# Cross-attention and gated feed-forward on one core: where the first keys are masked, how queries are normalised, and when the statistics are taken

## The reference, cut to what matters

```python
def _layernorm(x, axis=-1, eps=1e-05):
    m = jnp.mean(x, axis=axis, keepdims=True)
    v = jnp.var(x, axis=axis, keepdims=True)
    return (x - m) / jnp.sqrt(v + eps)
...
    qk = jnp.einsum('bhdq,bhdl->bhql', qh, kh) * scale
    sm = jax.nn.softmax(qk, axis=-1)
    ret = jnp.einsum('bhql,bhdl->bhdq', sm, vh)
...
    x = x + jnp.tanh(g_xattn[0]) * _L0_xattn_ref(_layernorm(x, axis=-1), ctx_2048, ctx_2048, L0_xattn_gamma)
    x = x + jnp.tanh(g_ffn[0]) * _L0_ffn_ref(_layernorm(x, axis=-1), ...)
```

## Time and profile before

| what | value |
|---|---|
| median of 3 runs | 214.7 us (214.63 to 214.72) |
| profiled execution, its own time | 213.49 us |
| span of its instructions | 211.7 us |
| mean granted clock of TensorE | 0.974 of full speed |
| busy: PE, DVE, POOL, ACT | 198.6, 159.3, 145.7, 125.0 us |

### The profile page before, as it was taken

How to read it: one execution, slowest core, us unless ns; L and a number is a source line. 1 busy time by engine, 2 the same in 40 slices (tenths; PEclk the granted TensorE clock), 3 DMA queues, 4 the chain that set the end, 5 groups by cost and what they waited for, 6 DMA issues and landing times.

```text
span 211.7 us, 4722 instructions
## 1 busy us (share of the span) xinstructions
PE 198.6 (94%) x1785; PEld 120.9 (57%) x1785; DVE 159.3 (75%) x336; ACT 125.0 (59%) x242; POOL 145.7 (69%) x167
## 2 busy tenths in 40 slices
PE   8569999999999999999999998999799999999991
PEld 5236456665665566556654553446566666766581
DVE  3799899999999997698968617055957676765985
ACT  2012758776877586768776774369547544854450
POOL 5994779957999999983799302384554899567440
PEclk9975899999999999999999999999999999999999
DMA  6799601101122231232311412311320003003033
GB/s 177 228 351 388 125 2 53 31 26 49 53 91 70 65 127 31 59 117 67 101 58 50 121 39 55 102 51 51 113 90 10 2 3 99 0 0 99 5 99 99
DMA packets 19783, 17.75 MB, mean 84 GB/s; under 512 B 4016, under 2 KB 19248, under 8 KB 19760
## 3 DMA queue, kind: packets, MB, share of 16 engines
q1 hardware_dynamic: 19760, 17.44, 26.6%
HBM read 11.02 MB, written 6.42 MB: 82 GB/s over the span
## 4 chain that ended last, share of the span: by engine, by line
PE 79%; DVE 12%; ACT 3%; issue 2%; POOL 1%; DMA 1%; SPq 0%; DVEq 0%; ACTq 0%; POOLq 0%
PE ps L727 19%; PE ps L791 17%; PE ps L768 13%; PE ps L739 12%; PE ps L852 9%; DVE neg_max L545 6%; PE ps L742 4%; PE ps L755 2%; PE ps L752 2%; ACT p_t L468 1%; DMA c_sb<-in_ctx 1%; PE ps L778 1%; ACT xn L497 1%; DVE p_t L701 1%; DVE p_t L696 1%
## 5 line engine op out<-in xcount | busy, mean ns | idle before, releaser
L545 DVE TENSOR_REDUCE neg_max<-ps 128x2 f32<-128x512 f32 x128 | 79.5, 683 | 11.8 <-PE ps L727 11.6
L468 ACT ACTIVATE p_t<-ps 128x512 f32<-128x512 f32 x128 | 66.9, 600 | 20.9 <-PE ps L742 18.9
L727 PE MATMUL ps<-km,qn 32*128 32x512 f32 x256 | 74.6, 651 | 3.7 <-POOL qn L351 3.2
L739 PE MATMUL ps<-qm,c_sb 32*128 32x512 f32 x256 | 74.6, 651 | 1.3 <-ACT p_t L468 1.3
L791 PE MATMUL ps<-w_exp,w_gu 128*128 128x512 f16 x192 | 45.2, 380 | 1.3 <-DVE w_exp L596 1.2
L434 POOL TENSOR_TENSOR f_lo<-fu,f_hi 128x512 fp32r<-128x512 f32 x23 | 29.3, 1279 | 21.5 <-ACT f_hi L486 21.5
L742 PE MATMUL ps<-max_t,sel 4*128 4x256 bf16 x256 | 35.1, 274 | 0.0
L742 PEld LDWEIGHTS ps<-max_t,sel 4*128 4x128 bf16 x256 | 18.8, 96 | 23.1 <-issue 20.7
L768 PE MATMUL ps<-p_t,v_t 128*32 128x256 f32 x512 | 30.9, 382 | 0.4 <-ACT p_t L468 0.4
L662 DVE SCALAR_TENSOR_TENSOR ga<-th,ps 128x512 f32<-128x512 f32 x24 | 16.4, 682 | 19.6 <-ACT th L481 19.6
L739 PEld LDWEIGHTS ps<-qm,c_sb 32*128 32x128 f32 x256 | 27.3, 188 | 5.8 <-issue 2.9
(11 more groups left out here) (69 smaller groups left out, 228.1 us busy)
## 6 DMA issues: line engine op xcount, KB each, us to landing
u_scr<-u_sb SPq DMA_DIRECT2D x32, 128.0 KB
u_n<-u_scr SPq DMA_DIRECT2D x16, 128.0 KB
r_n<-r_scr SPq DMA_DIRECT2D x16, 128.0 KB
out_x<-p_t SPq DMA_DIRECT2D x16, 128.0 KB, 1.9
x_sb<-in_x SPq DMA_DIRECT2D x3, 512.0 KB, 8.9
c_sb<-in_ctx SPq DMA_DIRECT2D x3, 512.0 KB, 8.9
w_all<-in_L_ffn_gate_w SPq DMA_DIRECT2D x1, 768.0 KB, 9.2
w_all<-in_L_ffn_up_w SPq DMA_DIRECT2D x1, 768.0 KB, 9.8
```

The lines of the kernel that those rows point to most:

```text
L468: nc.scalar.activation(p_t[:, b % 2, i, :], ps[:, bank_of["t", n][0], :], ACT.Exp, scale=DH ** -0.5).then_inc(exp_ok, 1)
L545: nc.vector.tensor_reduce(neg_max[:, b % 2, at:at + PAR, 0], ps[:, bank_of["s", n][0], :].rearrange("p (e l) -> p e l", e=PAR), axis=AX.X, ...
L727: nc.tensor.matmul(ps[:, bank, :], qn[rows, b % 2, P * t:P * (t + 1)], km[rows, b % 2].rearrange("p e l -> p (e l)"), start=True, stop=Tru ...
L739: nc.tensor.matmul(ps[:, bank, :], c_sb[rows, b, P * t:P * (t + 1)], qm[rows, b % 4].rearrange("p e l -> p (e l)"), start=True, stop=False)
```

## The change

Masking the first keys moves from POOL to DVE, which also computes the negated mean of batch 0; `km` of batch 0 has a semaphore of its own (`k0_ok`). POOL computes negated means for the later groups inside `pow_group` and normalises by adding the negated mean, where it subtracted the mean; `norm_apply_first` likewise uses the negated means of the second norm, which were there before. The masked queries become a function of their own, `masked(b)`; in the opening, `masked(0)` stands behind `queries(1)` and the clearing of `nm_parts`, and `masked(1)` behind the clearing of `v_t`. DVE's statistics are taken by the table `STATS`, for one to three batches at a time; `binades` and `rounded` get other steps, the scale products go from step 9 to step 11, and `pick` and `sel` stand behind the first keys. PE does 20 products ahead of the first scores, where it did 25.

```diff
--- before.py
+++ after.py
@@ -29,8 +29,9 @@
 E4M3_MIN_EXP = 2.0 ** -6
 E4M3_MAGIC = 1.5 * 2.0 ** 20
 HALF = HT * I // 2
-HALF_BINADES = (1, 2, 4, 5, 6, 8)
-HALF_ROUNDED = (2, 3, 5, 6, 7, 8)
+STATS = {0: (4, 6), 1: (6, 8), 4: (8, 11), 5: (11, 14), 7: (14, 15), 9: (15, 16)}
+HALF_BINADES = (2, 3, 6, 8, 9, 10)
+HALF_ROUNDED = (3, 4, 6, 8, 10, 11)
 
 
 def bank_table():
@@ -117,6 +118,7 @@
 
         stats = sb("stats", [P, NB, 6])
         mv = sb("mv", [P, NB, 2])
+        neg_m = sb("neg_m", [P, NB])
         veps = sb("veps", [P, NB])
         rstd = sb("rstd", [P, NB])
         stats2 = sb("stats2", [P, NB, 6])
@@ -186,8 +188,11 @@
         ag1_ok = sem("ag1_ok")
         v1_ok = sem("v1_ok")
         r1_ok = sem("r1_ok")
+        nm0_ok = sem("nm0_ok")
+        nm1_ok = sem("nm1_ok")
         qn_ok = sem("qn_ok")
         qm_ok = sem("qm_ok")
+        k0_ok = sem("k0_ok")
         k_ok = sem("k_ok")
         s_ok = sems("s_ok", NG)
         max_ok = sem("max_ok")
@@ -334,6 +339,8 @@
                 nc.gpsimd.tensor_scalar(veps[:, lo:hi], mv[:, lo:hi, 1], EPS, None, ALU.add).then_inc(v1_ok, 1)
                 pool.wait_ge(v1_ok, n + 1)
                 nc.gpsimd.tensor_tensor(rstd[:, lo:hi], veps[:, lo:hi], mhalf[:, 0:hi - lo], ALU.pow).then_inc(r1_ok, 1)
+                if n > 0:
+                    nc.gpsimd.tensor_scalar(neg_m[:, lo:hi], mv[:, lo:hi, 0], -1.0, None, ALU.mult).then_inc(nm1_ok, 1)
 
             def keys(b):
                 pool.wait_ge(masks_ok, 1)
@@ -346,10 +353,17 @@
 
             def queries(b):
                 pool.wait_ge(r1_ok, group_of(b) + 1)
+                if group_of(b) > 0:
+                    pool.wait_ge(nm1_ok, group_of(b))
+                else:
+                    pool.wait_ge(nm0_ok, 1)
                 if b >= 2:
                     pool.wait_ge(max_ok, FILLS * (b - 1))
-                nc.gpsimd.tensor_scalar(qn[:, b % 2, :], x_sb[:, b, :], mv[:, b, 0:1], rstd[:, b:b + 1],
-                                        ALU.subtract, ALU.mult).then_inc(qn_ok, 1)
+                nc.gpsimd.tensor_scalar(qn[:, b % 2, :], x_sb[:, b, :], neg_m[:, b:b + 1], rstd[:, b:b + 1],
+                                        ALU.add, ALU.mult).then_inc(qn_ok, 1)
+
+            def masked(b):
+                pool.wait_ge(masks_ok, 1)
                 if b >= 4:
                     pool.wait_ge(exp_ok, FILLS * (b - 3))
                 pool.wait_ge(qn_ok, b + 1)
@@ -357,16 +371,18 @@
                     nc.gpsimd.tensor_scalar(qm[:, b % 4, e, :], qn[:, b % 2, :], mask[:, e:e + 1], 1.0,
                                             ALU.mult, ALU.mult).then_inc(qm_ok, 1)
 
-            keys(0)
             pow_group(0)
             queries(0)
             keys(1)
             pow_group(1)
             queries(1)
             nc.gpsimd.memset(nm_parts[:], 0.0).then_inc(consts, 1)
+            masked(0)
             nc.gpsimd.memset(v_t[:].rearrange("p s t h c -> p (s t h c)"), 0.0).then_inc(consts, 1)
             pool.wait_ge(consts, 7)
             nc.gpsimd.memset(v_t[:].rearrange("p s t h c -> p (s t h) c")[:, :, 0:1], 1.0).then_inc(consts, 1)
+
+            masked(1)
 
             def rounded(k):
                 m, part = k // 2, slice(HALF * (k % 2), HALF * (k % 2 + 1))
@@ -399,8 +415,8 @@
             def norm_apply_first():
                 for t in range(CH):
                     q = t
-                    nc.gpsimd.tensor_scalar(xn2[:, q, :], x_sb[:, t, :], mv2[:, t, 0:1], rstd2[:, t:t + 1],
-                                            ALU.subtract, ALU.mult).then_inc(n2_ok, 1)
+                    nc.gpsimd.tensor_scalar(xn2[:, q, :], x_sb[:, t, :], neg_m2[:, t:t + 1], rstd2[:, t:t + 1],
+                                            ALU.add, ALU.mult).then_inc(n2_ok, 1)
 
             for b in range(NB):
                 if b + 2 < NB:
@@ -408,6 +424,7 @@
                         pow_group(group_of(b + 2))
                     keys(b + 2)
                     queries(b + 2)
+                    masked(b + 2)
                 if b in HALF_ROUNDED:
                     rounded(HALF_ROUNDED.index(b))
                 if b == 9:
@@ -528,9 +545,9 @@
 
         @block.vector
         def _(v):
-            def stats_group(n):
-                lo, hi = GROUPS[n]
-                v.wait_ge(x_in[n], 16)
+            def stats_batches(lo, hi):
+                v.wait_ge(x_in[group_of(lo)], 16)
+                v.wait_ge(x_in[group_of(hi - 1)], 16)
                 for b in range(lo, hi):
                     nc.vector.bn_stats(stats[:, b, :], x_sb[:, b, :]).then_inc(st1_ok, 1)
                 for b in range(lo, hi):
@@ -600,6 +617,13 @@
             v.wait_ge(consts, 4)
             nc.vector.tensor_reduce(mask[:], ident[:].rearrange("p (g e d) -> p e g d", g=NG, e=PAR),
                                     axis=AX.XY, op=ALU.add).then_inc(masks_ok, 1)
+            stats_batches(0, 1)
+            v.wait_ge(ag1_ok, 1)
+            nc.vector.tensor_scalar(neg_m[:, 0:1], mv[:, 0, 0:1], -1.0, None, ALU.mult).then_inc(nm0_ok, 1)
+            v.wait_ge(masks_ok, 1)
+            v.wait_ge(c_in[0], 16)
+            for e in range(PAR):
+                nc.vector.tensor_scalar(km[:, 0, e, :], c_sb[:, 0, :], mask[:, e:e + 1], None, ALU.mult).then_inc(k0_ok, 1)
             pairs = ident[:].rearrange("p (g r) -> p g r", g=NG)
             for e in range(PAR):
                 nc.vector.tensor_reduce(pick[:, e:e + 1], pairs[:, :, 2 * e:2 * e + 2], axis=AX.XY,
@@ -607,21 +631,20 @@
             v.wait_ge(sel_ok, 2)
             for e in range(PAR):
                 nc.vector.tensor_scalar(sel[:, e, :], ones_b[:], pick[:, e:e + 1], None, ALU.mult).then_inc(sel_ok, 1)
-            stats_group(0)
-            stats_group(1)
+            stats_batches(1, 4)
 
             def between(b):
                 if b == 0:
                     v.wait_ge(tanh_ok, 1)
                     nc.vector.tensor_tensor(c_att[:], tanhs[:, 0:1], gates[:, 2:3], ALU.mult).then_inc(coef_ok, 1)
-                if b in (0, 3, 7):
-                    stats_group({0: 2, 3: 3, 7: 4}[b])
+                if b in STATS:
+                    stats_batches(*STATS[b])
                 if b in HALF_BINADES:
                     binades(HALF_BINADES.index(b))
                 if b in (7, 11, 15):
                     v.wait_ge(coef_ok, 1)
                     reciprocals((b - 7) // CH)
-                if b == 9:
+                if b == 11:
                     v.wait_ge(scales_in, 48)
                     nc.vector.tensor_scalar(ds_row[:], ds_row[:], tanhs[:, 1:2], None, ALU.mult)
                     nc.vector.tensor_scalar(gs_half[:], gs[:], 0.5, None, ALU.mult).then_inc(coef_ok, 1)
@@ -719,7 +742,10 @@
                 b, i = divmod(n, FILLS)
                 t, g = divmod(i, NG)
                 if i == 0:
-                    pe.wait_ge(k_ok, PAR * (b + 1))
+                    if b == 0:
+                        pe.wait_ge(k0_ok, PAR)
+                    else:
+                        pe.wait_ge(k_ok, PAR * b)
                     pe.wait_ge(qn_ok, b + 1)
                 bank, held = bank_of["s", n]
                 bank_free(held)
@@ -793,7 +819,7 @@
                 last.then_inc(gu_ok, 1)
 
             pe.wait_ge(idle_ok, 1)
-            for _ in range(25):
+            for _ in range(20):
                 nc.tensor.matmul(ps[:, RING - 1, 0:L], idle[:, 0:P], idle[:, 0:L], start=True, stop=True)
             pe.wait_ge(consts, 5)
             for n in range(LEAD - 3):
```

## The result

The changed kernel takes 224.14 us (median of 4 runs, 223.6 to 225.9), the kernel before 214.66 (median of 4). The ratio is 1.045, with a 95% interval of 1.040 to 1.051: slower by 4.5%, where 211.4 us were forecast and the range ended at 214.3. The span of the profiled execution (225.9 us) is 224.1 us.

A forecast was written before the change was run, and what follows sets the result against it. PE was taken to bound the middle, with losses in the opening, its low clock, one DVE overload and two late POOL places. Savings of 1.9 + 0.45 + 1.0 = 3.35 us gave 211.4 us, range 209.8 to 214.3.

The forecast's parts named there:

- The bounds of the kernel before: Whole kernel: PE limits the middle; exceptions are the opening, its low clock, DVE overloaded once (0.60 us), POOL late twice (0.30, 0.70).
- The addition, 0.48 us for a query: POOL's queries and first-chunk normalisations: adding a negated mean takes 0.48 us where subtracting took 1.236.
- The first rival: POOL's queries: the addition is no faster than the subtraction, so no change, 214.8 us; chance 0.21.
- Keys on DVE, first maximum at 6.8 to 6.9, turn 0 at 12.5: Opening: DVE masks batch 0's keys, bringing the first maximum from 8.10 and batch 0's turn from 13.69 to these times.
- Twenty products instead of 25: Opening, PE: they end at 5.3, just before the scores; 25 would end at 6.35, DVE hiding all but 0.2 to 0.3.
- The opening's sum, 1.9 us: Opening through turn 2: 1.9 us saved in all, bounds 1.2 to 2.9, with turn 2 at 28.45 instead of 30.3.
- The formula for turn 2: Opening: turn 2 comes at about turn 0's time plus 11.45 plus half of (X minus 12.8).
- X: Opening: the time at which TensorE's low clock ends, taken to move from 23.06 to 21.8 us.
- Statistics and `binades` in other steps: 0.45 saved: DVE's side work spread over steps with 1.8 us slack each: 0.6 us go, 0.1 to 0.2 come in step 9.
- The prediction's own sign of being wrong: DVE's steps: a side job in its new step holds a maximum by over 0.2 us in more steps than one.
- POOL's late places, 1.0 saved: Queries of batches 12 and 15: PE's stalls of 0.30 and 0.70 us both go, 1.0 saved.
- The one on the slow side: Opening: PE idles more, its low clock lasts much longer, through turn 2; 216.0 us; chance 0.07.

The follow-up runs named there:

- experiment 10: The changed kernel with POOL waiting for DVE's side work in steps 3, 6, 8, 9, 10 and 11, as in experiment 3, timed again: 209.85 us, ratio 0.981.
- experiment 4: The changed kernel with 25 instead of 20 products ahead of the first scores: 223.04 us, ratio 1.056.
- 1: The changed kernel with the attention's queries subtracting the mean again instead of adding its negative: 213.43 us, ratio to the kernel before 0.997.
- experiment 2: The kernel before, changed only so that POOL makes negated means and adds them, in queries and first-chunk normalisations: 223.89 us.
- experiment 3: The changed kernel with POOL waiting, ahead of its long instructions, for DVE's side work in steps 3, 6, 8, 9, 10 and 11: 211.56 us.
- 7: The kernel before with the addition alone, plus POOL waiting for DVE's side work in steps 2, 5, 6, 8 and 9: 216.34 us, ratio 1.015.
- 8: The changed kernel with no wait, POOL clearing an unused tile ahead of its long instructions in steps 3, 4, 6 and 8 to 11: 214.05 us, ratio 1.002.

## Why the prediction was wrong, point by point

- **The bounds of the kernel before**: right. The overload of step 7 and both places where POOL was late are gone in experiment 10, whose products of batches 0 to 12 stand 7.06 us apart throughout.
- **The addition, 0.48 us for a query**: right in kind, 0.552 measured. The first rival is refuted: adding took 0.55 us and subtracting 1.22. The Trainium skill ("GPSIMD Engine Reference", section 3.1) prices an element by how many operations the loop's body has (the same price up to two); with the two operations that either instruction names, that would make both equal, and the measurement decides. How many the engine's loop really has, no run shows. The operand changed with the operation (a column of `neg_m` for one of `mv`), and no run separates the two.
- **Keys on DVE, first maximum at 6.8 to 6.9, turn 0 at 12.5**: right; 6.61 and 12.20 measured. DVE's two masks took 0.62 us (0.6), and POOL's power beside them 0.58, with none of the 0.3 us added for contention. In no trace does a POOL power hold DVE: sixteen exponent instructions that started behind one of four columns took 0.55 to 0.56 us. So the earlier trace rows was a row of the one kind that could not show the cost.
- **Twenty products instead of 25**: the scores started at 5.47 with 20 and at 5.42 with 25 (experiment 4); so the 0.2 to 0.3 us of gain are not seen. In experiment 4's execution the products became faster early: 12 of them in the microsecond from 4, where the changed kernel did 6.
- **The opening's sum, 1.9 us**: mis-sized, by the clock; 0.21 measured. The formula for turn 2 came close: 12.2 + 11.45 + 6.8 = 30.5, measured 30.09; but X was 25.5, not 21.8. I had put the point at which the opening gains nothing at 25.5, and the changed kernel came to lie there. Where the clock is back early the formula says too little (28.15 measured in experiment 10, 27.5 by it); the chain between turns 1 and 2 is PE's there, 7.66 us at the full clock instead of 7.07, and why stays open.
- **Statistics and `binades` in other steps: 0.45 saved**: this is the step that failed, together with POOL's steps. I put side work into DVE's slack at the durations that it had before, 1.1 us a pair, and worked out POOL's steps by themselves. That the durations are those of the one who comes first wasn't in either sum. I priced the meeting of the two engines in one place only, in the opening, at 0.3 us, from a row in which DVE had come in second and still lost nothing; in the steps it costs 4.0 us (3) and 8.3 (9 to 11). The prediction's own sign of being wrong, a side job that holds a maximum by over 0.2 us in more steps than one, came true. The shared steps could be read from the two tables, and the order from rows: 2.63 against 3.51 us behind the start of `keys`, a margin of 0.88 from which the addition takes 0.67 and the stretch of POOL's small instructions the rest. The gains themselves were sized right: experiment 10 is 1.46 us faster than the kernel before from batch 0 to batch 12, where 0.45 and 1.0 were forecast.
- **The rule**: the Trainium skill ("SBUF — State Buffer", section "SBUF: two separate sides") calls the shared pair of ports an exclusive lock that the first to start holds for the whole instruction. The prediction cited it and let it change 0.2 us. The traces agree with it for POOL's rounding and attention: 2.05 to 2.62 us for instructions of 0.55 where POOL's had just begun, less where it was nearly through (1.02 in step 10), and 0.55 to 0.79 in the kernel before, where DVE came ahead of the long ones. They do not agree for every instruction: the powers hold nothing, and the subtracting `qn` of batch 8 in the kernel before, in flight from 58.66 to 60.18, let an exponent instruction of 0.79 us start at 59.12 and end at 59.91.
- **POOL's late places, 1.0 saved**: right (nothing idle there after), and swallowed by the rest.
- **The sum without the holding** was 210.15 us for a profiled execution; experiment 10 measured 209.88. That is partly luck: its opening gave 2.1 us with a low stretch of 6.8 us, and the same kernel's gave 0.4 in experiment 3, with 13.7.
- **The rivals**: none held the mechanism. The one on the slow side had the opening's clock as its cause. That clock took the opening's gain and not more; later low stretches, in steps 3 and 9, followed TensorE's idle time behind the holdings.

Shown by runs: that the order of arrival is the loss up to batch 12 (1, 2, 3, 7, 8 and 10 from both sides), and that neither the table nor the opening is. Not shown by any run: that the ports are what is shared, which is the page's account. What decides how long TensorE's clock stays low stays open.

## What to carry to other kernels

Where two engines exclude each other, as here, the duration of an instruction depends on who starts first, so make the order part of the schedule: let the one whose long instructions are off the path wait for the short ones that are on it, by a semaphore and not by a margin of tenths of a microsecond. Before an engine off the path is made faster, look for what it will then meet: here 0.7 us less for each query on POOL cost some 10 us by itself, and a wait in six steps turned the whole change from a loss of 4.5% into a gain of 1.9%.

## What was not expected of the hardware

- What holds and what does not: POOL's rounding, attention and masking, and its clearing, hold DVE's `tensor_scalar`; its power of four columns does not (0.55 to 0.56 us in sixteen cases), and DVE's maxima (0.68) and reciprocals (0.55) are not held by any.
- GpSimd's `tensor_scalar` of 128x256 float32: multiply and multiply 0.48 us, add and multiply 0.55, subtract and multiply 1.22, each with per-channel values.
- A DVE `tensor_scalar` of six columns takes 0.15 to 0.17 us alone and 1.77 behind a POOL instruction in flight (2.31 in experiment 2); a clearing on POOL, which reads nothing, also holds DVE (1.06 us instead of 0.55).
- The low stretch of TensorE's clock in the opening varies between executions of the same kernel: 13.7 us in experiment 3, 6.8 in experiment 10, with batch 0's weighted product at 28.09 and 26.36. Over all traces it is 3.4 to 13.7 us.
